# A Perceiver layer on one core: softmax sums of the self-attention taken with the exponentials, their reciprocals spread by identity products, two weight clips placed behind the maxima

## The chip, the core and the metric

The kernel runs on one core of one Trainium2 chip. The core has TensorE (PE, matrix products, into PSUM only), VectorE (DVE), ScalarE (ACT), GpSimd (POOL) and a queue that only starts DMAs (SP). Each engine works off its own instructions in order and waits for the others by semaphores. The metric is the time of one execution in microseconds (us), as the median of several runs.

## The reference

One layer on 256 tokens of width 512: cross-attention to 4096 keys, self-attention with 16 heads of 32, and a gated network with weights rounded to -1, 0, 1. The part that the change touches is the self-attention's softmax and the rounding of the weights:

```python
# self-attention, 16 heads, Dh = 32
scores = jnp.einsum('bhqd,bhkd->bhqk', Q, K) / jnp.sqrt(jnp.float32(Dh))
probs = jax.nn.softmax(scores, axis=-1)
ctx = jnp.einsum('bhqk,bhkd->bhqd', probs, V)
out = jnp.einsum('bsd,df->bsf', ctx, W_out)
return out + X

# network, three weights w1, w3 (512 x 1408) and w2 (1408 x 512)
def weight_quant(w):
    scale = 1.0 / jnp.clip(jnp.mean(jnp.abs(w)), EPS)
    return jnp.clip(jnp.round(w * scale), -1.0, 1.0) / scale
```

## The kernel before

There is no scheduler: every engine has one block of code, whose order is its order of work. The cross-attention takes the first 461 us and is left as it is; then come two layer norms, the projections to `qT`, `kT` and `v_sb`, the self-attention (about 495 to 525 us), the output product, a layer norm with rounding to 8 bits, and the network.

The self-attention goes by **units** v = 0 to 7 of two heads each. Two units make a **group** g of four heads, 128 channels of the context `cT`. For a unit the steps are:

- TensorE, `head_scores(v)` (L806): scores of two heads, queries on the partitions, into two PSUM banks of 4 to 7.
- VectorE, `maxima(v)` (L1404): the negated row maxima, `anm`.
- ScalarE, `exponentials(v)` (L1105): four exponentials of 128x256 (two heads x, two token tiles t) into `prob`.
- TensorE, `head_transposes(v)` (L818): eight transposes of 128x128 into banks 0 and 1, half by half.
- `probabilities_out(v)`: banks 0 and 1 are copied to `pT` (L1116 by ScalarE; L1410 by VectorE for units 0 to 2, L1113 by ScalarE from unit 3 on).
- TensorE, `head_products(v)`: `v_sb` times `pT` into the context's 32 rows for each head (L838), and, one unit later, a matrix of ones times the same `pT` (L847), which gives the softmax sum of each token, repeated on the head's 32 partitions. Group g has bank 2 + g % 2: context in the first half, sums in the second. `tile_position` puts a head's product in one of four column groups of the array.
- VectorE, `context_out(g)`: reciprocal of the 128x256 sums (L1418) and multiplication with the context (L1419) into `cT`. The last group does so in two halves.

TensorE's order is: transposes of v, scores of v+2, products of v-1. After the units, `wout_sb` times `cT` with the residual gives banks 6 and 7 (L869, L873), then ten products `keep_busy` (L589) that only occupy the array, then the transposes of the rounded `h2b` (L882) and the network.

Meanwhile GpSimd rounds the weights in eight pieces each: `weight_magic` (L546: scale and add a large number) and `weight_round` (L553: subtract it, into bf16). VectorE clips each rounded weight in one instruction, `clip(j)` (L1424, 128x5632 bf16). The clips of w1 and w3 stand in the units 2 and 3 of VectorE's loop; GpSimd waits for both (`wclip_done`, 2) before it begins w2. The network's first product waits for the clip of w1 (L908).

## Time and profile before

| | us |
|---|---|
| median of 3 runs | 561.07 |
| lowest, highest | 559.59, 561.34 |
| the profiled execution, whole | 562.67 |
| its span in the profile | 560.9 |
| TensorE busy in the span | 528.2 (94%) |
| VectorE busy | 469.7 (84%) |
| ScalarE busy | 366.6 (65%) |
| GpSimd busy | 159.0 (28%) |

The profile is of one execution, whose whole time is 1.60 us above the median of the timed runs. Times in the rows count from the start of the span. The busy shares are means over stages with different limits; about this change only the stretch from 495 us on says anything. In the timeline, rows of the same instruction that follow each other are merged (x8 is eight of them, and the time that of all). A bracket tells how long the engine stood idle before a row, and what released it. For TensorE the matrix product and the load of its weights (PEld) are rows of their own; an fp32 product of L838, L847, L869 and L873 is two records.

### The profile page before, as it was taken

The page shows a single profiled execution, that of the slowest core. Times are in us where ns is not written, and L with a number is a line of the kernel's source. Part 1 is how long each engine was busy: PE and PEld are TensorE (multiplying, and loading weights), DVE is VectorE, ACT ScalarE, POOL GpSimd, SP SyncE. Part 2 cuts the span into 40 slices and gives each one's busy share as a digit, 9 for nine tenths or more (in the row PEclk, how much of TensorE's full clock was granted, in tenths as well). Part 3 has the DMA queues.
Part 4 walks back from the last instruction along what each step waited for, and adds up shares of the span by engine and source line. Part 5 has one row for each costly group of instructions (what it writes and reads, how often), then busy time and mean ns, then how long its engine had stood idle before and what let it go on. Part 6 is the DMA issues. An engine that isn't in the chain of part 4 may idle for free.

```text
span 560.9 us, 10025 instructions
## 1 busy us (share of the span) xinstructions
PE 528.2 (94%) x3803; PEld 352.8 (63%) x3803; DVE 469.7 (84%) x708; ACT 366.6 (65%) x447; POOL 159.0 (28%) x202
## 2 busy tenths in 40 slices
PE   7899978799999999999999999999998998999996
PEld 4776743367667666667667666666676784455443
DVE  3569996999899999999999999999995447478686
ACT  2154335887886886786886886886885344886442
POOL 2579965002202202202202202202000001596500
PEclk9999999999999999999999999999997998999999
DMA  8999187699999999999999999999998997500001
GB/s 312 341 346 328 43 137 242 86 194 217 200 194 199 204 197 201 213 211 208 204 189 209 204 196 202 198 202 203 203 189 166 230 416 306 228 1 1 1 0 39
DMA packets 287806, 107.41 MB, mean 192 GB/s; under 512 B 276896, under 2 KB 277920, under 8 KB 286368
## 3 DMA queue, kind: packets, MB, share of 16 engines
q1 hardware_dynamic: 287776, 107.01, 88.1%
q8 instruction: 18, 0.29, 0.2%
q14 instruction: 12, 0.10, 0.1%
HBM read 37.26 MB, written 0.52 MB: 67 GB/s over the span
## 4 chain that ended last, share of the span: by engine, by line
PE 63%; DVE 22%; DMA 5%; ACT 4%; issue 3%; POOL 1%; SPq 0%; ACTq 0%; DVEq 0%; POOLq 0%
PE ps L662 16%; PE ps L664 8%; PE ps L644 8%; PE ps L646 8%; PE ps L645 8%; DMA pT<-split 5%; DVE rows L1270 4%; PE ps L764 3%; DVE split L1252 3%; PE ps L693 2%; DVE qrot L1308 2%; DVE qrope L1302 2%; DVE KL L1290 2%; DVE qrot L1305 1%; PE ps L873 1%
## 5 line engine op out<-in xcount | busy, mean ns | idle before, releaser
L662 PE MATMUL ps<-pT,VH 128*128 128x256 f16 x1024 | 196.8, 274 | 2.1 <-DMA pT<-split 1.9
L664 PE MATMUL ps<-pT,VL 128*128 128x128 f16 x1024 | 183.4, 220 | 0.0
L1270 DVE TENSOR_SCALAR_CACHE_REDUCE rows<-ps,qback 128x1024 f32<-128x1024 f32 x128 | 163.6, 1280 | 15.6 <-PE ps L646 15.5
L1030 ACT ACTIVATE split<-rows,rz 128x2048 f16<-128x2048 f32 x64 | 124.8, 1995 | 67.5 <-DVE rz L1218 65.6
L1252 DVE SCALAR_TENSOR_TENSOR split<-rows,rz,split 128x2048 f16<-128x2048 f32 x64 | 150.3, 2350 | 1.3 <-issue 1.2
L662 PEld LDWEIGHTS ps<-pT,VH 128*128 128x128 f16 x1024 | 100.6, 98 | 42.6 <-DMA pT<-split 4.4
L1016 ACT ACTIVATE rows<-rows,negm 128x2048 f32<-128x2048 f32 x64 | 127.2, 1989 | 0.2 <-DVE negm L1275 0.2
L664 PEld LDWEIGHTS ps<-pT,VL 128*128 128x128 f16 x1024 | 100.6, 98 | 27.7 <-issue 0.3
L525 POOL TENSOR_TENSOR ctx_c<-acc 128x128 f32<-128x128 f32 x32 | 24.4, 761 | 298.0 <-ACT acc L1005 298.0
L644 PE MATMUL ps<-KH,qcur 128*128 128x512 f16 x256 | 97.1, 379 | 3.3 <-DVE rows L1270 3.3
L646 PE MATMUL ps<-KH,qcur 128*128 128x512 f16 x256 | 97.0, 379 | 0.0
L645 PE MATMUL ps<-KL,qcur 128*128 128x512 f16 x256 | 97.0, 379 | 0.0
L646 PEld LDWEIGHTS ps<-KH,qcur 128*128 128x128 f16 x256 | 25.0, 98 | 30.2
L495 POOL TENSOR_TENSOR qrope<-qrope,qrot 128x384 f32<-128x384 f32 x32 | 39.2, 1244 | 12.3 <-DVE qrot L1308 12.3
L644 PEld LDWEIGHTS ps<-KH,qcur 128*128 128x128 f16 x256 | 25.1, 98 | 10.2 <-DVE rows L1270 4.3
L693 PE MATMUL ps<-hTq,wq_sb 128*128 128x256 f32 x128 | 29.6, 384 | 1.5 <-ACT hTq L943 0.8
L693 PEld LDWEIGHTS ps<-hTq,wq_sb 128*128 128x128 f32 x128 | 23.7, 190 | 6.9 <-issue 2.9
L645 PEld LDWEIGHTS ps<-KL,qcur 128*128 128x128 f16 x256 | 25.0, 98 | 2.2
L1302 DVE TENSOR_TENSOR qrope<-ps,qcos_sb 128x768 f32<-128x768 f32 x16 | 15.2, 950 | 13.1 <-PE ps L704 13.0
L704 PE MATMUL ps<-qhk,wkcq_sb 128*128 128x256 f32 x96 | 23.8, 387 | 1.2 <-DVE qrot L1308 1.2
L546 POOL TENSOR_SCALAR w_sb<-w_sb,wscale 128x704 f32<-128x704 f32 x24 | 20.5, 875 | 14.1 <-DVE wscale L1380 9.8
L704 PEld LDWEIGHTS ps<-qhk,wkcq_sb 128*128 128x128 f32 x96 | 17.6, 190 | 5.7 <-issue 3.3
(175 smaller groups left out, 641.0 us busy)
## 6 DMA issues: line engine op xcount, KB each, us to landing
w_sb<-w SPq DMA_DIRECT2D x3, 2816.0 KB, 15.8
wq_sb<-wq SPq DMA_DIRECT2D x4, 1024.0 KB, 10.2
wo_sb<-wo SPq DMA_DIRECT2D x16, 256.0 KB, 4.5
wkcq_sb<-wkcq SPq DMA_DIRECT2D x4, 768.0 KB, 10.3
keys<-ctxT SPq DMA_DIRECT2D x8, 256.0 KB, 11.3
stage<-ctxT SPq DMA_DIRECT2D x16, 128.0 KB, 10.0
stage<-kcos SPq DMA_DIRECT2D x8, 256.0 KB, 10.0
stage<-ksin SPq DMA_DIRECT2D x8, 256.0 KB, 10.7
```

The costliest lines, as they stand in the source:

```text
L495: nc.gpsimd.tensor_tensor(qrope[:, h % 4, part], qrope[:, h % 4, part], qrot[:, h % 2, part], ALU.add).then_inc(qrope_done, 1)
L644: nc.tensor.matmul(o, q[0], KH[:, key], start=True, stop=False)
L645: nc.tensor.matmul(o, q[0], KL[:, key], start=False, stop=False)
L646: last = nc.tensor.matmul(o, q[1], KH[:, key], start=False, stop=True)
L662: nc.tensor.matmul(bank(6 + r % 2, 0, 256), VH[:, 4 * b + k, :], p.rearrange("p x q -> p (x q)"), start=(b == 0 and k == 0), stop=False)
L664: last = nc.tensor.matmul(bank(6 + r % 2, 0, 128), VL[:, 4 * b + k, :], p[:, 0, :], start=False, stop=(b == 7 and k == 3))
L693: last = nc.tensor.matmul(bank(0, a * TOK, (a + 1) * TOK), wq_pair(wq_sb, q)[:, c, head], hTq[:, c, :], start=(c == 0), stop=(c == DK - 1))
L704: last = nc.tensor.matmul(ps[:, o:o + TOK], wkcq_sb[:, h // WQG % 2, h % WQG, c * 128:(c + 1) * 128], qhk[:, h, :], start=True, stop=True)
L1016: nc.scalar.activation(part, part, ACT.Exp, bias=negm[:, k:k + 1], accum_out=zpart[:, k, half:half + 1]).then_inc(exp_done, 1)
L1030: nc.scalar.activation(split[:, split_slot(r, half), :, 0, :], rows[:, k, half * 2048:(half + 1) * 2048].rearrange("p (b k) -> p b k", k=1 ...
L1252: nc.vector.scalar_tensor_tensor(out=split[:, split_slot(r, half), :, 1, :], in0=rows[:, k, half * 2048:(half + 1) * 2048].rearrange("p (b ...
L1270: nc.vector.tensor_scalar(rows[:, k, c * 1024:(c + 1) * 1024], ps[:, score_bank(s) * 512:(score_bank(s) + 2) * 512], qback[:, r // 2:r // ...
```

## The change

1. Each exponential also gives the sum of its row (`accum_out`), into `azs`: one number for each head and token. `head_reciprocals(v)`, on VectorE at the head of each unit's turn, takes the reciprocals of four such numbers a partition into `arz`.
2. The products with ones go, and with them the ninth call of `head_products`. In the odd units eight products with the identity come instead ("spread"): a column of `arz`, repeated over 32 weight columns, times the identity gives the reciprocals along the tokens on the head's 32 partitions, in bank 3.
3. `context_out(g)` copies the spread from PSUM to `ainv` and multiplies the context with it. It stands after the reciprocals of units 3, 5 and 7, before the maxima.
4. The contexts of even and odd groups now share bank 2, the spreads bank 3. The first products of group g wait for the context of group g-1 (before: g-2). The copies to `pT` wait for the products of unit v-3 (before: v-2).
5. `clip` of w1 and w3 moves behind the maxima of unit 7 and to the next turn, and GpSimd no longer waits for them before w2.
6. The sum of w2 (`weight_sum(2)`) stands ahead of the scores of unit 4 on TensorE.

```diff
--- before.py
+++ after.py
@@ -106,7 +106,9 @@
         qkn = at("qkn", EF + 20 * KB, [128, TT, 2, DM])
         prob = at("prob", C, [128, 4, 2, TT, TOK])
         pT = at("pT", C + 20 * KB, [128, 6, TT, TOK])
-        arz = at("arz", EF + 24 * KB, [128, 2, TOK])
+        azs = at("azs", EF + 24 * KB, [128, UNITS, 2, TT])
+        arz = at("arz", EF + 24 * KB + 128, [128, AH, TT])
+        ainv = at("ainv", EF + 25 * KB, [128, 2, TOK])
         PT_UNITS = 3
         BOTH_FROM = 3
         w1_sb = at("w1_sb", A + 32 * KB, [128, DK * FF])
@@ -558,7 +563,6 @@
             weight_magic(1, w3_sb)
             pool.wait_ge(wround_done, WPIECES)
             weight_round(1, w3_sb, w3b)
-            pool.wait_ge(wclip_done, 2)
             weight_magic(2, w2_sb)
             weight_round(2, w2_sb, w2b)
             for t in range(TT):
@@ -822,31 +826,31 @@
             def head_products(v):
 
                 g, first = v // 2, v % 2 * 2
-                if v < UNITS:
-                    if first == 0:
-                        wait(pe, cT_done, g - 1)
-                    if v == 0:
-                        pe.wait_ge(v_copied, 2)
-                    if v == 2:
+                if first == 0:
+                    wait(pe, cT_done, g)
+                if v == 0:
+                    pe.wait_ge(v_copied, 2)
+                if first > 0:
+                    pe.wait_ge(arz_done, v + 1)
+                    wait(pe, ainv_done, g)
+                    if g == 0:
                         pe.wait_ge(wmean_done, 3)
+                    for t in range(TT):
+                        o = 3 * 512 + g % 2 * TOK + t * 128
+                        for a in range(HPG):
+                            last = nc.tensor.matmul(ps[a * DH:(a + 1) * DH, o:o + 128],
+                                                    arz[:, 4 * g + a, t:t + 1].broadcast_to([128, DH]), ident[:, :],
+                                                    start=True, stop=True, tile_position=(0, a * DH))
+                    last.then_inc(aspread_done, 1)
+                for x in range(2):
+                    pe.wait_ge(pT_done[x], v + 1)
+                for k in range(TT):
                     for x in range(2):
-                        pe.wait_ge(pT_done[x], v + 1)
-                for k in range(TT):
-                    if v < UNITS:
-                        for x in range(2):
-                            a = first + x
-                            last = nc.tensor.matmul(ps[a * DH:(a + 1) * DH, (2 + g % 2) * 512:(2 + g % 2) * 512 + TOK],
-                                                    v_sb[:, k, (4 * g + a) * DH:(4 * g + a + 1) * DH],
-                                                    pT[:, v % PT_UNITS * 2 + x, k, :],
-                                                    start=(k == 0), stop=(k == TT - 1), tile_position=(0, a * DH))
-                    if v >= 1:
-                        u = v - 1
-                        o = (2 + u // 2 % 2) * 512 + TOK
-                        for x in range(2):
-                            a = u % 2 * 2 + x
-                            last = nc.tensor.matmul(ps[a * DH:(a + 1) * DH, o:o + TOK], ones[:, 0:DH],
-                                                    pT[:, u % PT_UNITS * 2 + x, k, :],
-                                                    start=(k == 0), stop=(k == TT - 1), tile_position=(0, a * DH))
+                        a = first + x
+                        last = nc.tensor.matmul(ps[a * DH:(a + 1) * DH, 2 * 512 + g % 2 * TOK:2 * 512 + (g % 2 + 1) * TOK],
+                                                v_sb[:, k, (4 * g + a) * DH:(4 * g + a + 1) * DH],
+                                                pT[:, v % PT_UNITS * 2 + x, k, :],
+                                                start=(k == 0), stop=(k == TT - 1), tile_position=(0, a * DH))
                 last.then_inc(aav_done, 1)
 
             head_scores(0)
@@ -854,14 +858,13 @@
             keep_busy(9, 2)
             for v in range(UNITS):
                 head_transposes(v)
+                if v == 2:
+                    weight_sum(2, bank(3, 0, 1))
                 if v + 2 < UNITS:
                     head_scores(v + 2)
-                if v == 2:
-                    weight_sum(2, bank(3, 0, 1))
                 if v >= 1:
                     head_products(v - 1)
             head_products(UNITS - 1)
-            head_products(UNITS)
 
             pe.wait_ge(wout_in, 16)
             for t in range(TT):
@@ -1103,11 +1106,12 @@
                     for t in range(TT):
                         k = 2 * x + t
                         nc.scalar.activation(prob[:, v % 4, x, t, :], bank(4 + v % 2 * 2 + x, t * TOK, (t + 1) * TOK),
-                                             ACT.Exp, bias=anm[:, v, k:k + 1]).then_inc(aexp_done, 1)
+                                             ACT.Exp, bias=anm[:, v, k:k + 1],
+                                             accum_out=azs[:, v, x, t:t + 1]).then_inc(aexp_done, 1)
 
             def probabilities_out(v):
 
-                wait(act, aav_done, v - 1)
+                wait(act, aav_done, v - 2)
                 if v >= BOTH_FROM:
                     act.wait_ge(apT_done, 2 * v + 1)
                     nc.scalar.activation(pT[:, v % PT_UNITS * 2].rearrange("p k t -> p (k t)"), bank(0), ACT.Copy)\
@@ -1406,18 +1410,25 @@
             def probabilities_out(v):
 
                 dve.wait_ge(apT_done, 2 * v + 1)
-                wait(dve, aav_done, v - 1)
+                wait(dve, aav_done, v - 2)
                 nc.vector.tensor_copy(pT[:, v % PT_UNITS * 2].rearrange("p k t -> p (k t)"), bank(0)).then_inc(pT_done[0], 1)
 
+            def head_reciprocals(v):
+
+                dve.wait_ge(aexp_done, 4 * v + 4)
+                nc.vector.reciprocal(arz[:, 2 * v:2 * v + 2, :], azs[:, v]).then_inc(arz_done, 1)
+
             def context_out(g):
 
-                o = (2 + g % 2) * 512
-                dve.wait_ge(aav_done, 2 * g + 3)
+                o = 2 * 512 + g % 2 * TOK
+                dve.wait_ge(aspread_done, g + 1)
+                nc.vector.tensor_copy(ainv[:, g % 2, :], ps[:, o + 512:o + 512 + TOK]).then_inc(ainv_done, 1)
+                dve.wait_ge(ainv_done, g + 1)
+                dve.wait_ge(aav_done, 2 * g + 2)
                 for part in ([slice(0, TOK)] if g < FG - 1 else [slice(t * 128, (t + 1) * 128) for t in range(TT)]):
                     n = part.stop - part.start
-                    link(nc.vector.reciprocal(arz[:, g % 2, part], ps[:, o + TOK + part.start:o + TOK + part.start + n]))
-                    nc.vector.tensor_tensor(cT[:, g, part], ps[:, o + part.start:o + part.start + n], arz[:, g % 2, part],
-                                            ALU.mult).then_inc(cT_done, 1)
+                    nc.vector.tensor_tensor(cT[:, g, part], ps[:, o + part.start:o + part.start + n],
+                                            ainv[:, g % 2, part], ALU.mult).then_inc(cT_done, 1)
 
             def clip(j, wb):
                 dve.wait_ge(wround_done, WPIECES * (j + 1))
@@ -1427,6 +1438,9 @@
             maxima(0)
             maxima(1)
             for v in range(UNITS):
+                head_reciprocals(v)
+                if v in (3, 5, 7):
+                    context_out(v // 2 - 1)
                 if v < BOTH_FROM:
                     probabilities_out(v)
                 if v == 2:
@@ -1435,10 +1449,8 @@
                     maxima(v + 2)
                 if v == 1:
                     weight_total(2)
-                if v in (2, 3):
-                    clip(v - 2, (w1b, w3b)[v - 2])
-                if v in (3, 5, 7):
-                    context_out(v // 2 - 1)
+                if v in (5, 6):
+                    clip(v - 5, (w1b, w3b)[v - 5])
             context_out(FG - 1)
             clip(2, w2b)
```

VectorE, from the maxima of unit 4 (before) and of unit 7 (after) on; `anm` are the maxima, `w1b` and `w3b` the clips, `arz` reciprocals, `cT` the context. Before:

```order
L1404 TENSOR_REDUCE anm<-ps 128x4 [waits ascore_done]
L1424 TENSOR_SCALAR w1b<-w1b 128x5632 [waits wround_done]
L1404 TENSOR_REDUCE anm<-ps 128x4 [waits ascore_done]
L1424 TENSOR_SCALAR w3b<-w3b 128x5632 [waits wround_done]
L1418 RECIPROCAL arz<-ps 128x256 [waits aav_done]
L1419 TENSOR_TENSOR cT<-ps,arz 128x256 [waits dve_chain]
L1404 TENSOR_REDUCE anm<-ps 128x4 [waits ascore_done] x2
L1418 RECIPROCAL arz<-ps 128x256 [waits aav_done]
L1419 TENSOR_TENSOR cT<-ps,arz 128x256 [waits dve_chain]
```

After:

```order
L1408 TENSOR_REDUCE anm<-ps 128x4 [waits ascore_done]
L1435 TENSOR_SCALAR w1b<-w1b 128x5632 [waits wround_done]
L1419 RECIPROCAL arz<-azs 128x4 [waits aexp_done]
L1435 TENSOR_SCALAR w3b<-w3b 128x5632 [waits wround_done]
L1419 RECIPROCAL arz<-azs 128x4 [waits aexp_done]
L1425 COPY ainv<-ps 128x256 [waits aspread_done]
L1430 TENSOR_TENSOR cT<-ps,ainv 128x256 [waits aav_done,ainv_done]
L1425 COPY ainv<-ps 128x256 [waits aspread_done]
L1430 TENSOR_TENSOR cT<-ps,ainv 128x128 [waits aav_done,ainv_done]
L1430 TENSOR_TENSOR cT<-ps,ainv 128x128
```

The two clips stood between maxima; now they stand behind the last maxima and ahead of the reciprocals of units 6 and 7 and the contexts of groups 2 and 3.

TensorE, from the transposes of unit 7 on (L818, after: L822), then the products of unit 6, which are the first of group 3. Before:

```order
L818 MATMUL ps<-ident,prob 128x128 [waits pT_done0,aexp_done]
L818 MATMUL ps<-ident,prob 128x128 x3
L818 MATMUL ps<-ident,prob 128x128 [waits pT_done1,aexp_done]
L818 MATMUL ps<-ident,prob 128x128 x3
L838 MATMUL ps<-pT,v_sb 32x256 [waits pT_done1,pT_done0,cT_done]
L838 MATMUL ps<-pT,v_sb 32x256
L847 MATMUL ps<-pT,ones 32x256 x2
L838 MATMUL ps<-pT,v_sb 32x256 x2
L847 MATMUL ps<-pT,ones 32x256 x2
```

After:

```order
L822 MATMUL ps<-ident,prob 128x128 [waits pT_done0,aexp_done]
L822 MATMUL ps<-ident,prob 128x128 x3
L822 MATMUL ps<-ident,prob 128x128 [waits pT_done1,aexp_done]
L822 MATMUL ps<-ident,prob 128x128 x3
L850 MATMUL ps<-pT,v_sb 32x256 [waits pT_done1,pT_done0,cT_done]
L850 MATMUL ps<-pT,v_sb 32x256 x3
L841 MATMUL ps<-ident,arz 32x128 [waits ainv_done,arz_done]
L841 MATMUL ps<-ident,arz 32x128 x7
L850 MATMUL ps<-pT,v_sb 32x256 [waits pT_done1,pT_done0]
L850 MATMUL ps<-pT,v_sb 32x256 x3
```

The products with ones have gone from between the value products; the spread of group 3 stands between the products of units 6 and 7, and the wait for `cT_done` ahead of unit 6 is now for the third group's context instead of the second's.

## Rows read from the trace of the kernel before

**Rows 1.** Windows: length, busy us (count) of PE, PEld, DVE, ACT, POOL, then clock.

```profile
507.00:513.70 6.70, 6.70 (x74) 4.29 (x77) 6.46 (x7) 3.99 (x10) 2.61 (x4) 1.00 0.01 2
513.70:519.20 5.50, 3.82 (x44) 2.07 (x36) 5.47 (x6) 3.26 (x9) 5.35 (x7) 1.00 0.00 0
```

**Rows 2.** Chain of waits, in order of time: start us, us, what.

```profile
503.63 0.99 PE ps L838 x8
...
508.69 2.41 DVE w1b L1424
...
512.22 1.53 DVE w3b L1424
...
524.69 0.86 PE ps L847 x10
...
536.51 0.24 PE ps L882 x4
```

**Rows 3.** Timeline of self-attention's end and after: start us, us, engine, line, operation.

```profile
515.50 1.13 PE L806 MATMUL ps<-kT,qT 32*128 32x256 f32 x8
...
515.79 2.35 DVE L1404 TENSOR_REDUCE anm<-ps 128x4 f32<-128x1024 f32 x2
...
517.04 1.57 ACT L1105 ACTIVATE prob<-ps,anm 128x256 f32<-128x256 f32 x4 [2.24 <-DVE anm L1404]
...
519.25 1.12 PE L818 MATMUL ps<-ident,prob 128*128 128x128 f32 x8 [1.61 <-ACT pT L1113]
...
521.68 1.12 PE L818 MATMUL ps<-ident,prob 128*128 128x128 f32 x8 [0.32 <-ACT pT L1113]
...
525.48 1.12 PE L869 MATMUL ps<-x_sb,ident 128*128 128x512 f32 x2
...
534.47 0.43 DVE L1452 TENSOR_SCALAR h2b<-h 128x512 bf16<-128x512 f32 x1
```

**Rows 4.** Timeline, TensorE: block of unit 2 with ones-products, and next transposes.

```profile
510.19 0.41 PE L838 MATMUL ps<-pT,v_sb 128*32 128x256 f32 x2
...
511.19 1.09 PE L818 MATMUL ps<-ident,prob 128*128 128x128 f32 x8
```

**Rows 5.** Groups by shape, 495 to 531: count, busy us, mean ns, idle.

```profile
L1410 DVE COPY pT<-ps 128x512 f32<-128x512 f32 x3 | 2.1, 688 | 0.8 <-PE ps L818 0.8
...
L1419 DVE TENSOR_TENSOR cT<-ps,arz 128x256 f32<-128x256 f32 x3 | 1.3, 425 | 0.1
...
L1380 DVE RECIPROCAL wscale<-wmean 128x1 f32<-128x1 f32 x1 | 0.2, 164 | 0.0
```

**Rows 6.** Timeline, ScalarE: 128x256 from PSUM, plain (L968) and with sum (L970).

```profile
61.78 0.39 ACT L968 ACTIVATE QF<-ps 128x256 f32<-128x256 f32 x1 [1.34 <-PE ps L728]
62.07 0.38 ACT L970 ACTIVATE qabsolute<-ps 128x256 bf16<-128x256 f32 x1
62.33 0.20 ACT L970 ACTIVATION_READ_ACCUMULATOR qabsolute<-ps 128x1 f32 x1
62.42 0.39 ACT L968 ACTIVATE QF<-ps 128x256 f32<-128x256 f32 x1
```

**Rows 7.** Timeline, ScalarE: first exponentials and the copy of unit 1.

```profile
498.20 3.03 ACT L1105 ACTIVATE prob<-ps,anm 128x256 f32<-128x256 f32 x8 [0.58 <-DVE anm L1404]
...
504.34 0.69 ACT L1116 ACTIVATE pT<-ps 128x512 f32<-128x512 f32 x1
```

**Rows 8.** Timeline: rounding of w3, clip of w1, scaling of w2.

```profile
503.63 5.98 POOL L553 TENSOR_SCALAR w3b<-w_sb 128x704 bf16<-128x704 f32 x8
...
508.61 2.49 DVE L1424 TENSOR_SCALAR w1b<-w1b 128x5632 bf16<-128x5632 bf16 x1
...
513.85 6.67 POOL L546 TENSOR_SCALAR w_sb<-w_sb,wscale 128x704 f32<-128x704 f32 x8 [4.24 <-DVE w3b L1424]
```

**Rows 9.** Windows, TensorE: length, busy us (count), granted clock, DMA share, GB/s.

```profile
466.50:470.50 4.00, 1.66 (x7) 1.00 0.76 239
470.50:474.00 3.50, 3.50 (x5) 0.52 1.02 438
```

More of the change, by code:

```diff
@@ L200, in program @@
         aav_done = sem("aav_done")
+        arz_done = sem("arz_done")
+        ainv_done = sem("ainv_done")
+        aspread_done = sem("aspread_done")
         aexp_done = sem("aexp_done")
```

## The prediction

> **What bounds the kernel now.** I read the windows first, then the chain of waits, then the timeline of the stretch that changes. Everything before 498 us is left as it is, so the question is how long the eight units of the self-attention take, and whether what follows moves with them. The windows say that from 507.00 to 513.70 TensorE is busy the whole 6.70 us, and that it then works only 3.82 of 5.50 us [rows 1]. The chain of waits runs through VectorE in the middle: maxima, clip of w1 2.41, maxima, clip of w3 1.53, then a reciprocal of 128x256 [rows 2]. But the timeline shows what this lateness costs: TensorE goes on without a gap until the scores of unit 7 (515.50 to 516.56), and only then stands 1.61 us before the transposes of unit 6 and 0.32 us before those of unit 7, because the maxima of unit 6 began at 515.79 and their exponentials at 517.04 [rows 3]. At the end 8 of the 10 merged ones-products run alone, 0.86 us [rows 2]. From 525.48 on (first matmul of the output product) TensorE is the path by itself: products, then ten matmuls of `keep_busy` until 536.51, while VectorE has its `h2b` at 534.90 [rows 2, 3]. Both hang on the output product, and VectorE's side has 1.6 us to spare. So whatever moves the start of the output product (525.48) moves the end by the same amount, and I count everything to that point.
>
> **The sum's frame.** The profiled execution took 562.67 us: span 560.9 and 1.77 around it. That is 1.60 above the median 561.07. I work out a difference in the span and put it on the median.
>
> **What goes.** At most the two stalls (1.61 + 0.32) and the last ones-products (0.86): 2.8 us. The other ones-products were free: unit 0, whose block has none, takes 0.99 us [rows 2], unit 2's block with eight more records 1.00 us from its first product to the next transposes (510.19, 511.19) [rows 4]. They ran beside the value products in the other column groups. On VectorE the reciprocals of 128x256 go; in their place stand a reciprocal of four numbers (a [128,1] one is 164 ns; I take 170) and a copy of 128x256 out of PSUM. The multiplication of the same shape takes 425 ns, a copy of 512 columns 688, half of which is the lower bound; I take 420 [rows 5].
>
> **What comes, 1: accumulator reads.** Each of 32 exponentials now carries a sum, which is an instruction of its own behind it. The nearest row has the same shape: the plain 128x256 `QF` is followed 0.29 us later by the next instruction (61.78 to 62.07), the one with the sum 0.35 later (62.07 to 62.42), which is 0.09 after its read begins (62.33) [rows 6]. Bounds 0.06 and, if nothing overlaps, the read's own 0.20; I take 0.09. Where does it lie on the path? The second half of unit 2's transposes waits for ScalarE's copy of unit 1 (504.34, ends 505.03), which stands behind twelve exponentials from 498.20 on, with ScalarE at work all the time [rows 7]. So 12 x 0.09 = 1.1 us, less 0.1 of slack, reach TensorE: +1.0. From unit 4 on ScalarE waits for maxima (before unit 6's exponentials 2.24 us [rows 3]), which covers 0.36 a unit.
>
> **What comes, 2: spreads.** Four blocks of eight 128-column f32 products (weights: a column of `arz` repeated 32 times). If four column groups run at once, as value and ones products do, the eight need half of what eight 256-column products take (0.86): 0.43. If they run one by one, sixteen passes (two records a product) of about 0.11, 1.75. I take 0.55, the first with a little for the change of block, since the groups overlap in [rows 4]. Two of them stand before the scores of unit 7: +1.1. Gaps of 0.2 us that TensorE had there absorb a part. The scores of unit 7 then end at 516.56 + 1.0 + 1.1 - 0.2 = 518.5.
>
> **What is moved: the clips, and who is behind them.** On VectorE the clips of w1 and w3 now come after the maxima of unit 7. Behind them in VectorE's queue stand the reciprocals of units 6 and 7 and `context_out(2)`. And the products of unit 6 (group 3) now wait for `cT_done` 3, thus for `context_out(2)`; before they waited for group 1 only. The two contexts share bank 2 now, so this wait is part of the new layout. The Trainium skill, "PSUM — Partial Sum Buffer", section "PSUM bank collisions raise a hardware error", says that TensorE and another engine may not touch one bank and quadrant together; this case's trace can't show it, and the sum doesn't use it.
>
> From 518.5: maxima 1.14, clip, reciprocal 0.17, clip, reciprocal 0.17, copy 0.42, multiplication 0.43, links 0.1. The clip's price is the unknown. Unhindered it is 1.53 on the chain (w3); the clip of w1, same size, took 2.41 there. It was issued at 508.61 while GpSimd was rounding; GpSimd's last piece ended at 509.61, and 509.61 to 511.10 is just an unhindered clip [rows 8]. Before, GpSimd stood still during the second clip, since w2 waited for `wclip_done`. That wait is gone: GpSimd goes straight on at 509.61 with 6.67 us of scaling and, as for w3, 5.98 of rounding [rows 8], and is busy until about 522.3, over both clips. I take 2.41 for each. Then the products of unit 6 start at 518.5 + 7.25 = 525.75, while TensorE has had nothing to do since about 523.3: maxima of unit 7 until 519.7, its four exponentials 2.0, the copies of unit 6 0.5 and 0.6, the second half of the transposes 0.5. Behind them come 1.0, the last spread 0.55 and unit 7's 1.0: output product at 528.3 against 525.48, **+2.8 us**. `context_out(3)` and the third clip are not late: the group is needed 3.4 us after the output product starts and comes 0.3 after the products, the clip (1.6) ends before the first statistics 4.6 us later.
>
> By the Trainium skill, "SBUF — State Buffer", section "Who interferes with whom", whichever of VectorE and GpSimd issues first gets the shared port for its whole instruction and the other blocks. By that rule a clip waits for one GpSimd piece (0.74) at most, 2.27 us each, and the sum would be +2.5. The row of 508.61 speaks rather for more: the last of the eight pieces began at about 508.86, after the clip's own issue, and the clip waited through it.
>
> **The rivals.**
> 1. *The clips meet no hindrance.* For it: only one row shows the hindrance. Then 1.53 each: unit 6's products at 524.0, still after the transposes, and +1.1: 562.2.
> 2. *GpSimd is never let go of.* The w1 clip got in only when GpSimd had ended. If so here, the first clip ends at 523.8, the second at 525.5, unit 6's products start at 526.6: +3.7, 564.8.
> 3. *TensorE's clock falls in the new stall.* Between 466.50 and 470.50 TensorE was busy 1.66 of 4 us, and from 470.5 to 474.0 the granted clock was 0.52, the level of 1.2 GHz, which costs 1.7 us of full-rate work [rows 9]. The stall of 1.61 us had no such effect: its stretch shows 1.00 [rows 1]. The new stall is 2.4 us. If it falls: 563.9 + 1.8 = 565.7. The Trainium skill, "TensorE: Matmul & The Clock Gate", names activity as what keeps the clock up; the rows agree, and the sum doesn't rest on it.
> 4. *The other side: faster.* It decides on whether unit 6's products wait for VectorE at all. If reads and spreads hide (0 and 0.3 us each) and the clips cost the queue nothing beyond the cover of unit 5 to 7's work, the 2.8 us that go outweigh 1.2: -1.6, 559.5. Against it: with my 0.09 and 0.55 and no clips at all, unit 6's products would follow the transposes at 523.3, and the output product would start at 525.85: +0.4.
> 5. *Spreads run one by one*, 1.75: +6.4, 567.5. Against it the overlap in [rows 4].
>
> The change can't fail to do what it says: sums and products are written out.
>
> **How the numbers follow.** Forecast 563.9, chance 0.45; rival 1 0.17; rival 2 0.13; rival 3 0.14; rival 4 0.07; rival 5 0.04. A measurement of this kernel can tell some 0.3%, 1.7 us, from no change. Rival 1 and a part of rival 4 are within it, and so is a tenth of the forecast: same 0.24; faster 0.05; slower 0.71. The bounds of the unknowns: reads 0.06 and spreads 0.43 take 0.7 off, reads 0.13 and spreads 1.0 add 1.9. The range 561.7 to 567.0 takes in rival 1 with little to spare, rivals 2 and 3, and the dear spread; it leaves out rivals 4 and 5 and the rim of rival 1.
>
> **What would show it.** In the profile after: an ACTIVATION_READ_ACCUMULATOR of about 0.2 us behind each exponential, with unit 2's transposes about 1 us later; a spread block of 0.5 us; no stall before unit 6's transposes; both clips after the last maxima, 2.2 to 2.5 us each with GpSimd busy beside them; TensorE idle some 2.4 us before unit 6's products, released by `cT`; the output product some 2.8 us later than 525.48, and the distance from it to the end unchanged. The forecast is wrong if the clips take 1.6, if that idle time is missing, or if the clock row after it is under 1.

## The result and the profile after

| | before | after |
|---|---|---|
| median of 17 runs each, us | 560.6 | 567.15 |
| lowest, highest | 559.09, 565.45 | 562.5, 570.64 |
| the profiled execution: whole, span | 562.67, 560.9 | 564.63, 562.5 |

The ratio is 1.0098, 95% interval 1.0075 to 1.0122: the change costs 5.5 us (4.2 to 6.8). The two medians alone would give 1.0117, the means of the 17 runs (561.06 and 566.65) 1.010. The forecast was +2.8 us. The direction was right and the place too, but the size is about double. The profiled execution of after is one of the quicker ones (564.63 where the median is 567.15); a part of the cost can't be seen in it.

The work ahead of the self-attention takes some microseconds more or less from one execution to the next: in the profiles of this document the first exponential starts between 493.95 and 502.01. So I measure from the first exponential (497.06 after; 498.20 before, [rows 7]). Two distances matter: the **head**, from there to the first product of the output, and the **tail**, from that product to the end of the span. Before: head 525.48 - 498.20 = 27.28 [rows 3, 7], tail 35.42. After: head 30.03, tail 35.41. So +2.75 in the head, nothing in the tail.

Timeline of after, TensorE without weight loads; the bracket is the idle time ahead of a row and its releaser:

```profile
505.11 0.63 PE L822 MATMUL ps<-ident,prob 128*128 128x128 f32 x4 [0.40 <-ACT pT L1120]
...
506.85 0.64 PE L841 MATMUL ps<-ident,arz 128*32 128x128 f32 x16
507.32 1.03 PE L850 MATMUL ps<-pT,v_sb 128*32 128x256 f32 x8
...
515.90 1.13 PE L810 MATMUL ps<-kT,qT 32*128 32x256 f32 x8
...
517.95 1.09 PE L822 MATMUL ps<-ident,prob 128*128 128x128 f32 x8
...
520.90 1.11 PE L822 MATMUL ps<-ident,prob 128*128 128x128 f32 x8 [0.42 <-ACT pT L1117]
524.99 0.84 PE L850 MATMUL ps<-pT,v_sb 128*32 128x256 f32 x6 [2.97 <-DVE cT L1430]
525.45 0.41 PE L841 MATMUL ps<-ident,arz 128*32 128x128 f32 x4
525.66 0.39 PE L850 MATMUL ps<-pT,v_sb 128*32 128x256 f32 x2
525.87 0.50 PE L841 MATMUL ps<-ident,arz 128*32 128x128 f32 x10
526.13 0.39 PE L850 MATMUL ps<-pT,v_sb 128*32 128x256 f32 x2
526.20 0.28 PE L841 MATMUL ps<-ident,arz 128*32 128x128 f32 x2
...
527.09 1.13 PE L872 MATMUL ps<-x_sb,ident 128*128 128x512 f32 x2
```

The first row is the second half of unit 2's transposes: 8.05 behind the first exponential. Before it was 6.94 (505.14 - 498.20); there the eight transposes are one row, and the weight loads of the second half show its start:

```profile
505.14 0.42 PEld L818 LDWEIGHTS ps<-ident,prob 128*128 128x128 f32 x4 [0.17 <-issue]
```

A spread takes 0.47 (506.85 to 507.32). The 1.61 ahead of unit 6's transposes [rows 3] is gone (517.95 has no bracket). In its place stand 2.97 ahead of unit 6's products. Who makes them wait is on VectorE, in the same stretch:

```profile
517.08 1.22 DVE L1408 TENSOR_REDUCE anm<-ps 128x4 f32<-128x1024 f32 x1 [1.44 <-PE ps L810]
518.23 4.26 DVE L1435 TENSOR_SCALAR w1b<-w1b 128x5632 bf16<-128x5632 bf16 x1
522.40 0.16 DVE L1419 RECIPROCAL arz<-azs 128x4 f32<-128x4 f32 x1
522.49 1.59 DVE L1435 TENSOR_SCALAR w3b<-w3b 128x5632 bf16<-128x5632 bf16 x1
524.00 0.16 DVE L1419 RECIPROCAL arz<-azs 128x4 f32<-128x4 f32 x1
524.09 0.39 DVE L1425 COPY ainv<-ps 128x256 f32<-128x256 f32 x1
524.51 0.42 DVE L1430 TENSOR_TENSOR cT<-ps,ainv 128x256 f32<-128x256 f32 x1
```

And on GpSimd (scaling, then rounding of w2):

```profile
508.41 6.65 POOL L551 TENSOR_SCALAR w_sb<-w_sb,wscale 128x704 f32<-128x704 f32 x8
515.02 5.98 POOL L558 TENSOR_SCALAR w2b<-w_sb 128x704 bf16<-128x704 f32 x8
```

The first clip takes 4.26 us. GpSimd's stream ends at 515.02 + 5.98 = 521.00, the clip 1.49 later. The second, with GpSimd idle, takes 1.59. In the kernel before, the clip of w1 ended 1.49 behind GpSimd too (511.10 and 509.61, [rows 8]). The maxima at 517.08 take 1.22 beside a busy GpSimd: it is the clip that waits, not VectorE as such.

ScalarE, the first exponentials of after, each with its read:

```profile
497.06 0.47 ACT L1108 ACTIVATE prob<-ps,anm 128x256 f32<-128x256 f32 x1 [0.58 <-DVE anm L1408]
497.43 0.19 ACT L1108 ACTIVATION_READ_ACCUMULATOR prob<-ps,anm 128x1 f32 x1
497.52 0.47 ACT L1108 ACTIVATE prob<-ps,anm 128x256 f32<-128x256 f32 x1
```

The next one starts 0.09 behind the start of the read, as in [rows 6]. The reads themselves grow to 0.31 by unit 3, and that costs nothing: the exponentials still follow each other every 0.45 us. The last read of unit 3:

```profile
506.47 0.31 ACT L1108 ACTIVATION_READ_ACCUMULATOR prob<-ps,anm 128x1 f32 x1
```

The idle time did not lower the clock in this execution (windows of TensorE: length, busy us (count), granted clock, DMA share, GB/s):

```profile
522.02:525.00 2.98, 0.01 (x2) 1.00 0.00 0
525.00:531.50 6.50, 6.50 (x43) 1.00 0.01 3
```

### The profile page after: what moved, and what is told of

It reads as the page before. It is cut to its first block, busy times and chain, and to the rows that moved or that the text cites. A ratio compares the mean times of both kernels' runs of the same rounds, so it can differ in the third digit from the quotient of the medians.

```text
span 562.5 us, 10069 instructions
## 1 busy us (share of the span) xinstructions
PE 528.3 (94%) x3803; PEld 352.6 (63%) x3803; DVE 466.5 (83%) x715; ACT 369.5 (66%) x479; POOL 159.1 (28%) x202
## 4 chain that ended last, share of the span: by engine, by line
PE 63%; DVE 21%; DMA 5%; ACT 4%; issue 4%; POOL 1%; SPq 0%; DVEq 0%; ACTq 0%; POOLq 0%
PE ps L666 16%; PE ps L668 8%; PE ps L648 8%; PE ps L650 8%; PE ps L649 8%; DMA pT<-split 5%; DVE rows L1274 4%; PE ps L768 3%; DVE split L1256 3%; PE ps L697 2%; DVE qrot L1312 2%; DVE qrope L1306 2%; DVE KL L1294 2%; DVE qrot L1309 1%; PE ps L876 1%
```

## The experiments

Each of 1 to 12 ran beside runs of the kernel before on the same chip (23 to 29 of them, medians 560.73 to 561.16). "Clock" is the mean of the granted clocks of a kernel's runs.

| kernel | ratio, 95% | clock (runs) | head | tail |
|---|---|---|---|---|
| before | 1 | 0.995 (29) | 27.28 | 35.42 |
| the change | 1.0098, 1.0075 to 1.0122 | 0.990 (17) | 30.03 | 35.41 |
| 1 the change again | 1.0104, 1.0059 to 1.0150 | 0.989 (6) | 31.92 | 36.08 |
| 2 clips back | 1.0006, 0.9984 to 1.0028 | 0.995 (12) | 27.44 | 35.36 |
| 3 wait ahead of scaling | 1.0178, 1.0149 to 1.0207 | 0.988 (6) | 27.39 | 43.22 |
| 4 idle time filled | 1.0063, 1.0038 to 1.0088 | 0.995 (7) | 30.03 | 35.33 |
| 5 clips last, w2 later | 1.0050, 1.0027 to 1.0073 | 0.994 (12) | 27.00 | 36.53 |
| 6 reads alone | 1.0046, 1.0017 to 1.0075 | 0.992 (12) | 28.40 | 35.36 |
| 7 clips alone | 1.0092, 1.0063 to 1.0122 | 0.990 (6) | 32.87 | 35.38 |
| 8 three clips last | 1.0006, 0.9985 to 1.0028 | 0.994 (12) | 27.01 | 35.36 |
| 9 three semaphores | 1.0010, 0.9989 to 1.0031 | 0.993 (12) | 27.24 | 35.35 |
| 10 copies of unit 1 | 0.9985, 0.9967 to 1.0002 | 0.995 (12) | 26.46 | 35.35 |
| 11 wait between | 1.0006, 0.9984 to 1.0029 | 0.996 (12) | 27.41 | 35.37 |
| 12 wait for one clip | one execution, 559.71 us | 0.997 (1) | 27.40 | 35.43 |

Head and tail are read from each profile as above: in 4, 529.07 - 499.04 and 564.4 - 529.07.

### 1. The same kernel again

> The changed kernel once more, for its clock. Theory A (two costs: VectorE's first clip gets in only when GpSimd's stream ends, which leaves TensorE idle about 3 us before the products of unit 6, and in most executions the granted clock falls behind that idle time): the idle time is again 2.8 to 3.2 us; where the mean clock of a run is about 0.988 the profile shows a stretch at half the clock behind it, of 3 to 4 us, that the kernel before doesn't have; ratio to before 1.009 to 1.011. Theory B (the falls that both kernels have, near 425 and 470 us, only vary from run to run): no fall behind the idle time in this profile either, and the mean clocks of the two kernels' runs are alike.

This profile has the fall. Windows of TensorE, columns as above:

```profile
515.60:519.70 4.10, 3.68 (x42) 1.00 0.00 0
519.70:522.70 3.00, 0.06 (x1) 0.76 0.00 0
522.00:522.70 0.70, 0.00 (x0) 0.50 0.00 0
522.70:528.90 6.20, 6.17 (x36) 0.57 0.01 3
528.90:534.00 5.10, 5.10 (x14) 1.00 0.00 0
```

The third row is the end of the second. The clips (4.26 and 1.59) and the idle time (2.97) are as in the first profile to 0.01 us, but the granted clock goes to 0.50, the level of 1.2 GHz, within the idle time and stays there for 6.8 us: 0.76 over 3.00 are 1.4 us at half, 0.57 over 6.20 another 5.3. The head is 1.89 and the tail 0.67 longer than in the first profile: 2.56 us for one fall. Theory A's shape holds, though the stretch at half clock is twice as long as the 3 to 4 us expected. That the fall behind this idle time comes in *most* executions isn't shown, since a timed run lists only its mean clock; that mean is 0.988 or less in 11 of the 17 executions of the change, and in 1 of the 23 of the kernel before that ran beside this experiment.

### 2. The clips back in units 2 and 3

```diff
-                if v in (5, 6):
-                    clip(v - 5, (w1b, w3b)[v - 5])
+                if v in (2, 3):
+                    clip(v - 2, (w1b, w3b)[v - 2])
...
+            pool.wait_ge(wclip_done, 2)
             weight_magic(2, w2_sb)
```

> The changed kernel with the two clips back in units 2 and 3 and GpSimd waiting for both before w2; sums, spreads and banks as changed. Theory A: the products of unit 6 follow the transposes of unit 7 without idle time, the idle time before the transposes of unit 6 (1.6 us before) comes back; output product +0.4 to +1.2 us against the kernel before, clock as before; time 1.001 to 1.003 of before. Rival C (reads and spreads are the cost, and the place of the clips is nothing): 1.008 to 1.010.

Head +0.16, ratio 1.0006: reads, spreads and new banks together are worth nothing measurable, as the stalls and ones-products that went pay for them. Rival C is out: the cost lies in the place of the clips, with GpSimd let go beside them (this edit takes back both; 3 and 11 part them). One detail missed: the idle time ahead of unit 6's transposes did not come back. An idle time of 0.38 ahead of unit 2's products turned up instead. The likely reason, which no run tests, is that VectorE no longer has a reciprocal of 1.74 us (513.68 in the trace of the kernel before) between the second clip and the maxima of unit 6.

### 3. GpSimd waits, ahead of the scaling

```diff
+            pool.wait_ge(wclip_done, 2)
             weight_magic(2, w2_sb)
             weight_round(2, w2_sb, w2b)
```

> The changed kernel with one line put back: GpSimd waits for both clips before it scales w2. The clips stay behind the maxima of unit 7. Theory A: both clips take 1.5 to 1.6 us each instead of 4.26 and 1.59, the first products of unit 6 start 2.5 to 2.7 us earlier, the idle time before them is 0.3 us or less, and there is no clock fall behind it: ratio to before 1.001 to 1.003. w2 is then rounded about 12.7 us after the second clip, near 534, in time for its product near 548. If the clips are not hindered by GpSimd but slow in themselves: no change against the changed kernel, 1.010.

Timeline of this kernel, rows of four engines:

```profile
516.05 1.62 DVE L1436 TENSOR_SCALAR w1b<-w1b 128x5632 bf16<-128x5632 bf16 x1
...
517.67 1.60 DVE L1436 TENSOR_SCALAR w3b<-w3b 128x5632 bf16<-128x5632 bf16 x1
...
519.37 6.64 POOL L551 TENSOR_SCALAR w_sb<-w_sb,wscale 128x704 f32<-128x704 f32 x8 [13.11 <-DVE w3b L1436]
...
520.18 0.84 PE L851 MATMUL ps<-pT,v_sb 128*32 128x256 f32 x6 [0.33 <-DVE cT L1431]
...
531.98 1.63 DVE L1436 TENSOR_SCALAR w2b<-w2b 128x5632 bf16<-128x5632 bf16 x1 [9.03 <-POOL w2b L558]
...
538.40 0.61 PE L886 MATMUL ps<-identb,h2b 128*128 128x128 bf16 x4 [5.09 <-DVE h2b L1465]
```

Half right. With GpSimd idle the clips take 1.62 and 1.60 and the head is 27.39: the 4.26 was GpSimd's doing. But the kernel is 1.8% slower than the kernel before. I had asked only when w2 is *multiplied* (near 548), and not what stands behind its clip: on VectorE it is the layer norm. VectorE waits 9.03 us for the rounding, and TensorE then 5.09. The clock fell there as well: 5.60 us at 0.50 from 538.4.

### 4. The idle time filled

```diff
                 head_transposes(v)
+                if v == UNITS - 1:
+                    keep_busy(11, 4)
```

> The changed kernel with eleven bf16 products of 128x512 that only occupy TensorE (about 2.4 us) put between the transposes of unit 7 and the products of unit 6, into the idle time of 2.9 us that the late context of group 2 leaves there. The work that waits is as late as before. Theory A (the granted clock falls behind that idle time in most executions, worth about 2 us of the median): the span at clock 1.00 stays (560 to 561), the mean clock of the runs rises from 0.990 to about 0.995, the level of the kernel before, and the median drops by 1.5 to 2.5 us against the changed kernel: ratio to before 1.005 to 1.007. Theory B (the falls lie elsewhere and only vary): mean clock about 0.990 and 1.010 as the changed kernel.

Timeline, TensorE: the filling, then unit 6's products.

```profile
523.84 2.56 PE L593 MATMUL ps<-identb 128*128 128x512 bf16 x11
526.97 0.84 PE L850 MATMUL ps<-pT,v_sb 128*32 128x256 f32 x6 [0.58 <-DVE cT L1432]
```

The head is again 30.03, so nothing is earlier. But the clock goes from 0.990 to 0.995, and the ratio from 1.0098 (and 1.0104) to 1.0063, 2.0 to 2.3 us less. The intervals of the two ratios overlap by a little; together with the clock column (0.988 to 0.990 in the four kernels with a new idle time of 3 to 5 us, which are the change, its repetition, 3 and 7; 0.992 to 0.997 in all others) Theory A is well supported. Theory B is out as a full account, though not as a background: kernels without a new idle time fall too, near 110, 425, 470 and 555 us, in some executions. In the profiles with a fall behind a new idle time (1, 3 and 7) there is none at those places, and in the first profile of the change there are two (0.74 over 425 to 430 us, 0.80 over 470 to 475) and none behind the idle time. So a profile alone can't tell an added fall from one that has moved; the mean clock over the runs does.

### 5. All clips out of the way, that of w2 later

```diff
-                if v in (5, 6):
-                    clip(v - 5, (w1b, w3b)[v - 5])
             context_out(FG - 1)
-            clip(2, w2b)
+            clip(0, w1b)
+            clip(1, w3b)
...
+            clip(2, w2b)
             dve.wait_ge(cw_done, TT)
```

> The changed kernel with all the clips out of the way: those of w1 and w3 behind the context of group 3, that of w2 behind the rounding of the two token tiles. GpSimd waits for none. Theory A: the context of group 2 is made at once, the products of unit 6 follow the transposes of unit 7 with no idle time, output product 2.9 to 3.1 us earlier than in the changed kernel, which is about 0.2 before that of the kernel before; the clips take 1.6 each, hidden beside the output product (its first statistics are needed 4.6 us after it starts); 1.000 of before. If Theory B or C holds: 1.004 or more.

Head 27.00, as expected (-0.28 to before). The tail is 1.1 longer. Timeline, VectorE:

```profile
539.56 1.62 DVE L1435 TENSOR_SCALAR w2b<-w2b 128x5632 bf16<-128x5632 bf16 x1
```

It stands ahead of the hidden layer's products on VectorE, and TensorE, released there by `hmid` and `hb`, waits 0.34 and 1.46 (before: none and 0.59). Another clip in a queue where there was no room.

### 6. The reads alone

```diff
+        azs = at("azs", EF + 26 * KB, [128, UNITS, 2, TT])
...
-                                             ACT.Exp, bias=anm[:, v, k:k + 1]).then_inc(aexp_done, 1)
+                                             ACT.Exp, bias=anm[:, v, k:k + 1],
+                                             accum_out=azs[:, v, x, t:t + 1]).then_inc(aexp_done, 1)
```

> The kernel before with one thing of the change: every exponential also gives its row's sum, which nothing reads; products with ones, reciprocals, clips and waits are as before. Theory A: 0.09 us for each exponential, the second half of unit 2's transposes 1.0 to 1.1 us later after the first exponential than in the kernel before (6.94), the idle time of 1.61 before unit 6's transposes stays, since VectorE is full there; output product +0.5 to +1.1: ratio 1.001 to 1.002. If the time outside the span (1.8 us before, 2.2 in the changed kernel) comes from the sums, it is 2.2 here. Rival C (reads and spreads are the cost of the change): 1.004 or more.

Timeline, TensorE, second half of unit 2's transposes:

```profile
503.49 0.63 PE L819 MATMUL ps<-ident,prob 128*128 128x128 f32 x4 [0.40 <-ACT pT L1118]
```

That is 8.05 behind the first exponential (495.44): +1.1, to the hundredth that of the full change. The head is +1.12: in the old layout nothing takes it back (1.36 and 0.68 idle ahead of units 6 and 7's transposes, 1.61 and 0.32 before). The time, 1.0046, is more than 1.1 us (1.002), which is just inside the interval. The excess lies with the clock: the two executions at a mean clock of 1.000 take 559.95 and 560.68, 1.2 us above the mean of the five such executions of the kernel before beside it (558.72 to 559.68), while the three at 0.985 take 566.37 to 567.90. The mean clock, 0.992, was low for a kernel with no new idle time, and the cause of that stays open.

### 7. The clips alone

```diff
-            pool.wait_ge(wclip_done, 2)
             weight_magic(2, w2_sb)
...
-                if v in (2, 3):
-                    clip(v - 2, (w1b, w3b)[v - 2])
+                if v in (5, 6):
+                    clip(v - 5, (w1b, w3b)[v - 5])
```

> The kernel before with one thing of the change: the clips of w1 and w3 behind the maxima of unit 7 and in the next turn, and GpSimd not waiting for them. Sums by ones-products and the banks stay. Theory A (a clip gets in only when GpSimd's stream of sixteen pieces has ended, near 522.3 on the scale of the trace before): the first clip lasts 5 to 7 us, the second 1.6; the context of group 1 behind the first clip is about 5 us late, with two contexts of 2.2 us behind it; output product 3 to 5 us later, and a clock fall behind the idle time in part of the executions: ratio 1.006 to 1.012. If the clips were harmless in the old layout, which waits for the context of two groups earlier: 1.000 or below, by up to 1.6 us (the idle time before unit 6's transposes).

Timeline, three engines:

```profile
511.92 5.96 POOL L553 TENSOR_SCALAR w2b<-w_sb 128x704 bf16<-128x704 f32 x8
...
513.36 6.01 DVE L1423 TENSOR_SCALAR w1b<-w1b 128x5632 bf16<-128x5632 bf16 x1
...
521.54 0.64 PE L837 MATMUL ps<-pT,v_sb 128*32 128x256 f32 x2 [4.75 <-DVE cT L1418]
```

The clip ends 1.49 behind GpSimd once more (519.37, 517.88), and TensorE stands 4.75. Behind it the clock falls here too (windows of TensorE, columns as above), so that a part of the head of 32.87 is the clock's:

```profile
516.80:521.50 4.70, 0.00 (x0) 0.85 0.00 0
521.50:527.00 5.50, 5.46 (x41) 0.51 0.01 3
```

Moved alone, the clips cost as much as the whole change, so the old banks, which wait for the context of two groups earlier, give no shelter: that context stood behind the clip too.

### 8. Three clips in a row at the end

```diff
-                if v in (5, 6):
-                    clip(v - 5, (w1b, w3b)[v - 5])
             context_out(FG - 1)
+            clip(0, w1b)
+            clip(1, w3b)
             clip(2, w2b)
```

> The changed kernel with all three clips behind the context of group 3, in a row (1.62 each, 4.8 us). In the run with two clips there and the third later, the output product came 0.28 us sooner after the first exponential than in the kernel before, but the stretch from there to the end took 36.5 us instead of 35.4, since the late clip of w2 stood ahead of the hidden layer's products on VectorE. Here the third clip ends about 1.0 us after the first statistics could start, and h2b has 1.4 us to spare: no idle time is added on TensorE, the last stretch takes 35.4 again, and the time is 1.1 us below that run: ratio 1.000 to 1.003 to before. If h2b's slack is smaller than the trace says, the transposes of h2b wait and it is 1.004.

Timeline, VectorE: the third clip and the first statistics.

```profile
525.30 1.62 DVE L1435 TENSOR_SCALAR w2b<-w2b 128x5632 bf16<-128x5632 bf16 x1
526.84 0.69 DVE L1171 BATCH_NORM_STATS2 st<-ps 128x6 f32<-128x512 f32 x1
```

The third clip ends at 526.92, about 0.7 behind the time at which the statistics could start (4.6 us after the output product at 521.64), and the tail is 35.36: the slack of h2b covers it. 1.0006.

### 9. Three more semaphores

```diff
         aav_done = sem("aav_done")
+        spare1 = sem("spare1")
+        spare2 = sem("spare2")
+        spare3 = sem("spare3")
```

> The kernel before with three more semaphores that nothing uses. In all kernels with the changed self-attention, time minus span is 2.16 to 2.19 us; in the kernel before, and where only the row sums or only the clips are changed, 1.82 to 1.84. They differ in three semaphores. If these are the cause: 2.16 to 2.19 here, with the same span, about 0.35 us or 0.06% slower. If it is the new instructions: 1.82.

Time minus span 1.81: not the semaphores. Nor is it the reads (1.84 in 6) or the clips (1.83 in 7). All kernels with the spreads, reciprocals and copies have 2.11 to 2.19 on average. What in them costs 0.35 us outside the span stays open.

### 10. Unit 1's copies on VectorE

```diff
                 nc.vector.tensor_copy(pT[:, v % PT_UNITS * 2].rearrange("p k t -> p (k t)"), bank(0)).then_inc(pT_done[0], 1)
+                if v == 1:
+                    dve.wait_ge(apT_done, 2 * v + 2)
+                    nc.vector.tensor_copy(pT[:, v % PT_UNITS * 2 + 1].rearrange("p k t -> p (k t)"), bank(1))\
+                        .then_inc(pT_done[1], 1)
```

On ScalarE the copy of unit 1 from bank 1 is left out; the rest is kernel 8.

> The kernel with all three clips last, and in unit 1 VectorE makes both copies to pT, where ScalarE made the second. The sums cost 1.1 us because ScalarE has no pause in units 0 to 2; the second half of unit 2's transposes waits 0.41 for its copy of unit 1. With it on VectorE, which stands idle 0.5 to 1.0 us there, that wait goes: output product 26.6 us after the first exponential instead of 27.01; span 0.4 below: 0.999 to 1.001 of before, too little to tell in the time, to be read in the trace. If VectorE's maxima of unit 3 come later by the copy and ScalarE waits for them: no gain.

Timeline, TensorE, the transposes of unit 2:

```profile
504.89 1.14 PE L822 MATMUL ps<-ident,prob 128*128 128x128 f32 x8
```

They run in one go and end 504.89 + 1.14 - 497.89 = 8.14 behind the first exponential; in the changed kernel 8.68 (505.11 + 0.63 - 497.06), in the kernel before 7.6. Half of what the reads took is back. The head is 26.46, 0.82 below before; with 0.37 more outside the span 0.45 is left. The ratio, 0.9985 (0.9967 to 1.0002), is the lowest of all, 1.1% below the change, but not told from the kernel before.

### 11 and 12. A gap in GpSimd's stream

The wait of 3 one line later, for both clips; in 12 for the first only (`wclip_done, 1`).

```diff
             weight_magic(2, w2_sb)
+            pool.wait_ge(wclip_done, 2)
             weight_round(2, w2_sb, w2b)
```

> The changed kernel with one line: GpSimd waits for both clips between the scaling and the rounding of w2, so that its stream has a gap when the maxima of unit 7 end. The run with the same wait ahead of the scaling had both clips at 1.6 us but w2 so late that its clip held up the layer norm. Theory A: the clips take 1.6 each, idle time before the products of unit 6 is 0.3, output product 27.4 after the first exponential, the rounding of w2 starts about 21.5 us behind the first exponential of unit 0 plus 3, ends 6 us later, and its clip ends at about the time of the first statistics, within h2b's slack: ratio 1.000 to 1.003. If a clip waits for anything but GpSimd's stream: 4.3 us as in the changed kernel, 1.010.

Timeline of 11:

```profile
520.90 1.62 DVE L1436 TENSOR_SCALAR w1b<-w1b 128x5632 bf16<-128x5632 bf16 x1
...
522.52 1.60 DVE L1436 TENSOR_SCALAR w3b<-w3b 128x5632 bf16<-128x5632 bf16 x1
...
525.02 0.84 PE L851 MATMUL ps<-pT,v_sb 128*32 128x256 f32 x6 [0.32 <-DVE cT L1431]
...
530.22 1.63 DVE L1436 TENSOR_SCALAR w2b<-w2b 128x5632 bf16<-128x5632 bf16 x1 [2.42 <-POOL w2b L558]
```

One line of GpSimd's program takes the cost away (1.0098 to 1.0006), and the added falls of the clock go with it (mean clock 0.996).

> As the run with the wait between scaling and rounding of w2, but GpSimd waits for the first clip only, and then starts eight rounding pieces (5.97 us) just ahead of the second clip, which stands behind a reciprocal of 128x4. If a clip gets in only when GpSimd's stream has ended: the first clip takes 1.6, the second starts 0.1 to 0.2 behind GpSimd's first piece and ends 1.49 after its last, so it lasts about 7.3 us, and TensorE stands idle about 6 us before the products of unit 6. If it waits for one piece at most: 2.3. If GpSimd, starting later than usual, finds the second clip already issued: 1.6, and GpSimd's first piece waits.

Timeline of 12:

```profile
517.55 1.60 DVE L1436 TENSOR_SCALAR w3b<-w3b 128x5632 bf16<-128x5632 bf16 x1
```

and GpSimd beside it:

```profile
517.64 2.15 POOL L558 TENSOR_SCALAR w2b<-w_sb 128x704 bf16<-128x704 f32 x1 [4.86 <-DVE w1b L1436]
```

The last of the three cases came: the second clip was issued 0.09 ahead of GpSimd's first piece and takes 1.60, and now the *piece* waits: 2.15 us where one of the eight takes 0.75 (5.98 / 8). So neither engine has precedence, as far as this one execution shows. Whoever is in stays in: one clip, or a whole run of pieces issued back to back.

## Why the prediction was right, and where it was short

**Right, in kind and size.** Reads: forecast +1.0 at unit 2's transposes, measured +1.1, again alone. The stall of 1.61 and the late ones-products go: they do. Unit 6's products wait for `context_out(2)`, behind both clips: 2.97, forecast 2.4. Output product: +2.8 forecast, +2.75 measured. Tail unchanged: 35.41 against 35.42. Of the three signs that the prediction gave for being wrong, the idle time is there. The other two came in part: one of the two clips takes 1.59, and the clock behind the idle time is 1.00 in the first profile but under 1 in the second (0.57).

**Right as a sum, through errors that cancel.** The scores of unit 7 start 18.84 behind the first exponential (before 17.30): +1.5, where 1.9 was forecast, since a spread takes 0.47 and not 0.55 and more of the gaps absorbed it. The clips were taken as 2.41 each, 4.82 in all; they took 4.26 and 1.59, 5.85. The other steps there were 0.25 shorter than counted, so that the stretch from the end of unit 7's scores to unit 6's products is 8.03 (516.96 to 524.99) and not 7.25. From unit 6's products to the output product I counted 2.55; it took 2.10 (524.99 to 527.09), because nearly all of the last spread ran beside the value products: it starts at 525.45, before the last two records of unit 6's products (525.66), and its own last two start at 526.20, behind the first of unit 7's (526.13; the weight loads of unit 7 begin at 526.02). So -0.4, +0.8 and -0.45 against the forecast. That they add up to nothing is luck.

**The step that failed: the clip's price.** "I take 2.41 for each" carried one observed delay over as if it were a property of the clip. The delay is the remainder of GpSimd's stream at the time of issue: clip end = end of stream + 1.49 in all seven profiles where the two overlap (before, after, 1, 2, 4, 7 and 9: 1.47 to 1.49). Rival 2 ("never let go of", 0.13) had that rule right, and the time too. Counted from the first exponential, it has the first clip end at 25.6 (523.8 - 498.20); measured is 25.43 (522.49 - 497.06). The forecast's own sum has 23.85. Its +3.7 was too much by 0.2 there, by 0.3 in the steps from that clip to unit 6's products, and by the 0.45 above. The row it rested on was in [rows 8] all along. The Trainium skill, "SBUF — State Buffer", section "Who interferes with whom", has the first issuer hold the shared port for its instruction; 12 agrees for a clip that came first, while the clips of 4.26 and 6.01 us, which waited 2.8 and 4.5 us (about four and six pieces of 0.75), go beyond it.

**What was missing: the clock, as an addition.** Rival 3 (0.14) had it on top of the forecast's own mechanism, as it came (565.7), but for every execution or none. It comes in a part of the executions: one of two profiles of the changed kernel shows it, at 2.56 us; by experiment 4 it is worth 2.0 us in the comparison. I had a stall of 1.6 us without a fall and one of 2.3 (with TensorE busy 1.66 of 4 us) with it [rows 1, 9], and took the new one, 2.4 by my sum, as safe. Added up: 2.75 + 2.0 + 0.35 = 5.1, of 5.5 measured (4.2 to 6.8). The 0.35 outside the span was in no term; its cause is open. The executions with a mean clock of 1.000 say much the same without experiment 4: three of the 17 of the change take 562.50, 562.56 and 563.72 us, and the six of the kernel before beside experiment 1 take 558.64 to 560.08, 3.5 us less on average (other runs, not side by side), where head and time outside the span give 3.1. The rest of the cost is in the executions with a lower clock. The median, 567.15, is 0.15 above the upper end of the range; scaled to the median the forecast was made from, 1.0098 x 561.07 = 566.6.

## What to carry to other kernels

A long VectorE instruction that competes with GpSimd, as the clip does here, has no duration of its own: read where GpSimd's run of back-to-back pieces ends, and add the rest of the instruction (1.49 us for the clip). If it must run there, give GpSimd one wait, at the boundary after which its work can still be late, and check on *every* queue what stands behind the thing that is thereby delayed (3 and 11 differ by one line and 1.7%). And an idle time of three microseconds on TensorE costs more than itself in some executions, so filling it can pay even though nothing gets earlier.

## What was unexpected of the hardware

- A waiting clip isn't let in between two GpSimd pieces: 6.01 us, of which 4.5 waiting, through six roundings (7). The other way round, a piece waits 1.4 us for a clip (12).
- VectorE's maxima of 128x1024 out of PSUM take 1.22 us with GpSimd busy (after) and idle (3), the copy of 128x256 out of PSUM 0.39 to 0.42 either way: GpSimd does not hold them up.
- An exponential with a sum costs 0.09 us more than its plain form (one follows the other every 0.45 us, before every 0.36), however long its read's row is (0.19 to 0.31).
- The same idle time of 2.97 us was followed by a clock of 1.00 in one execution, and of 0.50 for 6.8 us in another.
- Time outside the span rose by 0.35 us with the new self-attention, not with semaphores, reads or clips.
